# Key norms of a cross attention by one power on GpSimd, and idle products in a gap of TensorE

## What is computed

```python
x = x + jnp.tanh(g_xattn[0]) * _L0_xattn_ref(_layernorm(x), ctx, ...)
x = x + jnp.tanh(g_ffn[0])   * _L0_ffn_ref(_layernorm(x), ...)
x = x + jnp.tanh(g_xattn[1]) * _L1_xattn_ref(_layernorm(x), ctx, ...)   # window attention, 16 heads
x = x + jnp.tanh(g_ffn[1])   * _L1_ffn_ref(_layernorm(x), ...)          # 16 experts
x = x + jnp.tanh(g_xattn[2]) * _L2_xattn_ref(ctx, _layernorm(x), ...)
...
# in _L2_xattn_ref: 8 heads of 64
k = k / jnp.maximum(jnp.sqrt(jnp.sum(jnp.square(k), axis=-1)), 1e-12) * k_scale
```

## Time and profile before

| | |
|---|---|
| median of 3 runs | 826.67 us (825.04 to 827.05) |
| profiled execution, own time | 825.94 us |
| its span | 824.1 us |
| PE, PEld busy | 735.4 us (89%), 469.1 us (57%) |
| DVE, ACT, POOL busy | 615.2 us (75%), 438.3 us (53%), 347.0 us (42%) |
| mean granted clock of TensorE | 0.943 |

### The profile page before, as it was taken

One profiled execution on the slowest core, in us unless ns is written; L12 is line 12 of the kernel. 1 busy time (PEld: TensorE's weight loads), 2 busy tenths in 40 slices (PEclk: granted clock), 3 DMA queues, 4 the chain that ended last, 5 costly groups with the idle time before them and its releaser, 6 DMA issues.

```text
span 824.1 us, 15426 instructions
## 1 busy us (share of the span) xinstructions
PE 735.4 (89%) x5468; PEld 469.1 (57%) x5468; DVE 615.2 (75%) x1297; ACT 438.3 (53%) x739; POOL 347.0 (42%) x283
## 2 busy tenths in 40 slices
PE   3799999997886978998899999998899999898997
PEld 3577787776544465663455555563346666653443
DVE  4779999998878765567565566658689999516786
ACT  2656667677484433435444545432127776743674
POOL 0665555561523501640677787740242211102464
PEclk8999999999998878999999999999859999999999
DMA  8267767532424512206022333007736678101520
GB/s 208 75 205 252 252 198 227 173 117 72 98 67 131 160 51 76 86 29 177 3 79 78 104 100 101 6 10 103 128 71 131 124 126 165 37 2 64 180 78 12
DMA packets 50645, 89.71 MB, mean 109 GB/s; under 512 B 17427, under 2 KB 34779, under 8 KB 50099
## 3 DMA queue, kind: packets, MB, share of 16 engines
q1 hardware_dynamic: 50578, 88.83, 39.8%
HBM read 63.29 MB, written 25.52 MB: 108 GB/s over the span
## 4 chain that ended last, share of the span: by engine, by line
PE 29%; DVE 17%; POOL 2%; ACT 2%; issue 2%; DVEq 0%; POOLq 0%; ACTq 0%
DVE arena L2516 11%; PE ps L1165 9%; PE ps L1155 7%; PE ps L1334 3%; PE ps L1348 2%; DVE arena L1898 2%; POOL arena L1820 2%; PE ps L1270 2%; PE ps L1259 1%; ACT arena L1647 1%; PE ps L1201 1%; PE ps L1242 1%; PE ps L1313 1%; PE ps L1171 1%; PE ps L768 1%
## 5 line engine op out<-in xcount | busy, mean ns | idle before, releaser
L2516 DVE TENSOR_REDUCE arena<-ps 112x1 f32<-112x500 f32 x192 | 114.6, 670 | 9.0 <-PE ps L1242 9.0
L1820 POOL TENSOR_TENSOR arena<-arena 125x448 f32<-125x448 f32 x96 | 109.2, 1137 | 24.6 <-ACT arena L1606 20.7
L1898 DVE TENSOR_TENSOR arena<-ps,arena 128x448 f32<-128x448 f32 (+7 forms) x139 | 80.8, 612 | 37.5 <-ACT arena L1564 18.3
L1647 ACT ACTIVATE arena<-ps 125x896 f32<-125x896 f32 x96 | 87.2, 917 | 23.5 <-PE ps L1259 23.4
L1165 PE MATMUL ps<-arena 125*128 125x448 f32 (+1 forms) x208 | 97.2, 548 | 2.0 <-ACT arena L1606 1.5
L1606 ACT ACTIVATE arena<-arena,kbias 125x448 f32<-125x448 f32 x96 | 63.6, 668 | 65.4 <-DVE arena L1898 47.9
L1898 DVE TENSOR_TENSOR arena<-ps,rn 125x448 f32<-125x448 f32 x96 | 59.2, 618 | 47.0 <-PE ps L1155 42.1
L843 PE MATMUL ps<-w_k2h,arena 128*125 128x512 f16 x288 | 69.4, 392 | 11.6 <-ACT arena L1416 10.4
L1155 PE MATMUL ps<-arena 128*125 128x448 f16 (+3 forms) x312 | 76.5, 354 | 1.2 <-DVEq L1909 1.1
L1155 PEld LDWEIGHTS ps<-arena 128*125 128x125 f16 (+1 forms) x312 | 40.1, 133 | 54.8 <-issue 41.8
L1416 ACT ACTIVATE arena<-ps 125x512 f32<-125x512 f32 x96 | 55.4, 598 | 12.4 <-PE ps L843 9.8
(11 more groups left out here) (323 smaller groups left out, 1462.7 us busy)
## 6 DMA issues: line engine op xcount, KB each, us to landing
arena<-in_ctxT SPq DMA_DIRECT2D x8, 750.0 KB, 9.3
d_cln<-arena SPq DMA_DIRECT2D x8, 750.0 KB
d_clnT<-arena SPq DMA_DIRECT2D x8, 750.0 KB
d_k<-arena SPq DMA_DIRECT2D x24, 250.0 KB
d_v<-arena SPq DMA_DIRECT2D x24, 250.0 KB
arena<-d_clnT SPq DMA_DIRECT2D x8, 750.0 KB
arena<-in_ctx SPq DMA_DIRECT2D x8, 672.0 KB
arena<-d_cln SPq DMA_DIRECT2D x8, 672.0 KB
```

What stands on the lines that cost most here:

```text
L1647: act.activation(p3[t % 2].rearrange("p (k h) q -> p k (h q)", k=2), ps[0:KP, 2 * (t % 2):2 * (t % 2) + 2, 0:8 * S], ACT.Exp).then_inc(l3_ ...
L1820: ins = pool.tensor_tensor(psum2[p][0:rows], psum2[p][0:rows], pexp[(t + p) % 2][0:rows], ALU.add)
L1898: return dve.tensor_tensor(out, a, b, op)
L2516: dve.tensor_reduce(mx3[bn % 2][:, u % 2, u % 8 // 2, u // 8:u // 8 + 1], ps[0:TT, max_bank_of(bn, u), 0:500], AX.X, ALU.max).then_inc(l3_ ...
```

## The change

The square root on ScalarE and the reciprocal on VectorE go away. GpSimd makes `rn` to the power -0.5 in one instruction of 125 x 768, between `remainders(22)` and `remainders(23)`; the exponent is one column of `nhalf`, spread over the 768. VectorE waits for it ahead of the third layer's scaling. In front of `turn_probs1(3)` TensorE gets nine idle products into bank 1, behind a wait for VectorE to have read the last scores.

```diff
@@ tensor
             for i in range(NT):
+                if i == NT - 1:
+                    pe.wait_ge(l1_sr, NT)
+                    keep_clock(9, 1)
                 turn_probs1(i)
@@ scalar
             later(17, 18)
-            act.wait_ge(rn_sq, 1)
-            rn_flat = rn[:, :, :, :].rearrange("p b t h -> p (b t h)")
-            act.activation(rn_flat, rn_flat, ACT.Sqrt).then_inc(rn_sd, 1)
             later(19)
@@ gpsimd
-            remainders(22, 23)
+            remainders(22)
+            pool.wait_ge(rn_sq, 1)
+            rn_flat = rn[:, :, :, :].rearrange("p b t h -> p (b t h)")
+            pool.tensor_tensor(rn_flat, rn_flat, nhalf[0:KP, 0:1].broadcast_to([KP, B * KT * H8]), ALU.pow)\
+                .then_inc(rn_rt, 1)
+            remainders(23)
@@ vector
                 if i + 2 < NT:
                     shift1(i + 2)
-                if i == 2:
-
-                    dve.wait_ge(rn_sd, 1)
-                    ch.step(dve.reciprocal(rn_flat, rn_flat))
                 normalise1(i)
...
             signal(operand)
+
+            dve.wait_ge(rn_rt, 1)
 
             def scale2(b, p, t):
```

More of the change, by code:

```diff
@@ L449, in build @@
         acc_full, acc_used = sem("kv_sums_full"), sem("kv_sums_used")
-        rn_sq, rn_sd = sem("l2_key_squares"), sem("l2_key_norms")
+        rn_sq, rn_rt = sem("l2_key_squares"), sem("l2_key_norms")
         dve_s, pool_s = sem("dve_steps"), sem("pool_steps")
```

## The result

The changed kernel takes 924.77 us (922.73 to 925.21, 4 runs) against 826.86 us for the one before: a ratio of 1.1179, 95% interval 1.115 to 1.1208. It is 98 us slower. I had forecast 822.3 us, with 885 as the upper end of the range.

A forecast was written before the change was run, and what follows sets the result against it. The attention's end was taken as a chain slowed by idle TensorE and half clock. 5.2 us gained less 0.8 given back took 825.94 to 821.5 us profiled, plus 0.73 for the median: 822.3 us, range 820.5 to 885.

The forecast's parts named there:

- What bounds the stage: End of the attention: a chain where one engine works and others wait, TensorE idling 2.68 us, then at half clock.
- the reciprocal alone is worth little: VectorE's reciprocal, 299.13 to 304.08: delays the chain some 0.2 us at the low clock, 2.0 us at the full clock.
- The idle products: Nine before `turn_probs1(3)`: 2.15 us, 296.5 to 298.65, free, cutting TensorE's idle time from 2.68 to 0.5 us.
- The chain at the full clock and what is given back: From 299.15: VectorE's sum behind the attention 5.2 us sooner, 0.8 lost at the first expert products, gain 4.4 us.
- The third rival: Nothing to measure: clock falls anyway, 826.2, or the power shuts out the subtraction at 289.02, 828.6; chance 13%.
- The power: GpSimd behind `remainders(22)`: 0.9 us start plus 768 columns at 7 ns, 6.3 us, ending at 296.3, clear of VectorE.
- The upper end: GpSimd's power if paid wholly per column: 0.2 us a column, 157 us for 768.
- the other reading: The small power at 369.32 may have fetched its four columns at once and computed for the rest; no size given.
- Clear by 15 us: GpSimd's power was to end 15 us before the layer norm's power, needed at about 312.
- the second: Price per column, 0.1 to 0.2 us each: power takes 78 to 157 us, layer norm's power waits, 900 to 976; 19%.
- The first: The power shuts VectorE out at the subtraction of `shift1(3)` or `shift1(2)`: +9 to +58 us, 836 to 885; 27%.
- The Trainium skill: GpSimd or two-SBUF-input VectorE instruction, whichever starts first, keeps shared ports throughout; with a 6.3 us power, +1.9 us.

The follow-up runs named there:

- the 600 columns: Changed kernel with the power over only 600 of the 768 columns, norms capped at 0.7, the rest raw: 904.04 us, ratio 1.0896 to the kernel before.
- 512: Changed kernel with the power over only 512 of the 768 columns, norms capped at 0.7, the rest raw: 887.54 us, ratio 1.071 to the kernel before.
- 520: Changed kernel with the power over only 520 of the 768 columns, norms capped at 0.7, the rest raw: 884.1 us, ratio 1.0678 to the kernel before.
- the version with the reciprocal in three: Kernel before plus nine idle products, VectorE's reciprocal cut into three of 256 columns in its idle times: 821.46 us (0.9934), on another chip 823.86 us (0.995).

## Why the prediction was wrong, by its own steps

- **What bounds the stage** and **the reciprocal alone is worth little**: right (826.72 without it and without the idle products).
- **The idle products**: right in price and place (2.11 us, no cost). Alone they give nothing that can be told (826.54). The reciprocal then holds the chain, as said, and the clock falls during `out1(3)`, which I had not reckoned with.
- **The chain at the full clock and what is given back**: 4.4 us forecast; without the power 826.65 - 822.31 = 4.3 measured. That the total agrees is partly luck: up to the sum behind the attention it is 3.7 us instead of 5.2 (1.9 where the clock fell earlier), and of the 0.8 given back there is nothing in that trace (the first eight expert products take 3.25 us as before). The third rival, a clock that falls anyway a little later, had its part in this.
- **The power**: this is the step that failed. "I take 7 ns a column, between 2.1 and 25": it is 159 ns, and 123.6 us instead of 6.3. The upper end (0.2 us a column, 157 us) was the nearer one; its 27% too much comes from taking a product's start (0.19 us) where the power has 0.37 and no more. What led me astray was the row at 369.32: four instructions of VectorE not slowed, and a power ending 0.10 us behind them. I took that for a power that had been shut out until then, and so for columns under 25 ns. At 159 ns a column its four columns alone take 0.64 us, so it can't have stood shut out until 370.45. The powers of up to 544 columns left VectorE free while they ran, which fits the other reading that I had named, a power that fetches its columns at once and then computes, and had given no weight in the sum. The 0.10 us was chance.
- **"Clear by 15 us"** for the layer norm's power: it followed from the 6.3 us. What stood behind the power was late by 97 us, and this is what the result consists of.
- **The rivals**: the second, price per column, had the mechanism, with its place behind the power in GpSimd's queue. It had 19% and was left out of the range. The first had VectorE's stall at the right instruction, and the 600 columns show it costing 75 us; in the changed kernel it is covered. Its upper end is off by its own terms: at 70 ns a column 55 - 0.5 is +54.5 us, 881, not +58 and 885. That changes nothing here.
- **The Trainium skill** (SBUF — State Buffer, "SBUF: two separate sides"), by which the first to start keeps the shared ports for the whole instruction: for products the rows agree. For the power they do not: with up to 544 columns nothing was held, with 600 and 768 the second SBUF input was held until 82.6 to 82.9 us after the power's start, not for 97.0 and 123.6. Nor was the subtraction of `shift1(2)` shut out by the power behind the remainder: it took 1.87 us, as before.

What stays open: that GpSimd takes in 512 columns, computes them, and only then fetches the rest, with some tens of columns waiting in a queue, fits all seven widths (4 to 768), and was argued, not seen; it is put together after the theories ahead of 512 and 520 had missed. Why the four-column product is held behind 82.9 us I put down to the results being written then; no run separates reads from writes. What makes the clock fall earlier in some traces than in others is open too, and so is where the version with the reciprocal in three gets its 3 to 5 us.

## What to carry to other kernels

A price that a trace shows at one size alone can be all start or all columns, and a second size has to decide; until then the sum has to bear the dearer reading: here 4 columns at 1.0 us were 0.64 us of columns, and 768 were 122. Before moving work to an engine that looks idle, read its queue behind the gap: the gap was 26.7 us long, and the instruction behind it was one that the whole kernel waits for. Two changes that each give nothing (a hidden reciprocal, a filled idle time) can give something together, so they have to be costed together, the clock included. And a profile is one execution: with the same work of TensorE the stretch from subtraction to sum took 13.2 us in some traces and 14.9 in others.

## What the runs showed of the hardware

- A power on GpSimd costs 0.37 us and 159 ns a column, the same from 4 to 768 columns (1.01 us for 4, 41.11 for 256, 123.63 for 768, the last with about 1 us of waiting in it). VectorE's reciprocal of the same 768 columns takes 4.95 us, or 1.74 to 1.75 us for 256.
- VectorE's instructions with two inputs in SBUF ran freely beside a power of 544 columns or fewer (the subtraction, 1.22 to 1.23 us, at 7 us after its start), and were held until 82.6 to 82.9 us after its start by one of 600 or 768. The four-column product behind that point was held to the power's end (20.67 and 38.86 us); beside powers of 256 it kept its 0.17 us. With one input in PSUM the subtraction was free beside a power of 768 (294.73, 1.22 us). Such holds show in the profile as busy time of VectorE: its 91.7 us more are no work.
